# A transformer layer with routed experts on one core: shared chunks split 12 and 4 around the routed ones, and the final norm moved into the experts' block

## The chip, the core and the metric

One core of a Trainium2 chip runs the whole layer in one launch. The metric is device time in microseconds; the median of three runs of the kernel before is 2378.51 us (2376.24 to 2379.26). The profiled execution took 2377.52 us, of which the trace's span covers 2375.8. Engines are named TensorE (PE in the profile, its weight loads PEld), VectorE (DVE), ScalarE (ACT), GpSimd (POOL) and Sync (SP), which here only issues DMAs.

## The reference

`x` is (4, 2048, 256) float32, so there are 8192 tokens of width 256. What is computed:

```python
x = x + layernorm(attention(layernorm(x)))          # 16 heads, prefix mask
t = layernorm(x)                                    # the tokens
scores = softmax(t @ gate_w.T); idx = top_k(scores + gate_b, 2)
cw = sum(one_hot(idx, 8) * scores[idx])
a = swiglu((t @ w1.T + b1) * (t @ w3.T + b3))       # for each of 8 experts, F = 256
routed = sum_e cw_e * (a_e @ w2_e.T + b2_e)
shared = swiglu((t @ sw1.T + sb1) * (t @ sw3.T + sb3)) @ sw2.T + sb2
x = x + layernorm(routed + shared)
```

The products of the experts are float32 in accuracy: each is made of three passes, with operands split into a high and a low part (`_hi`, `_lo`).

## The kernel before

Tokens are worked on in chunks of 512 (`CH`), 16 in all (`NCH`), each as 4 tiles of 128. The stages are `prepare`, `project` (to 186 us), `attend` (to 1345), `attention_out` and `route` (to 1450), `experts` (to 2296) and `combine`.

`experts` runs 55 chunks (`NEC`), one step each, in one list for all engines: first 16 shared chunks (every token through the shared expert), then 39 routed ones (`ROUTED`), whose rows were sorted by expert. The steps are pipelined. In step c TensorE transposes the rows of chunk c+1 (`turn`, L293), makes three of four blocks of the hidden products (L1548), then the down product of chunk c-1 (L304), then the fourth block. ScalarE and VectorE evict the blocks, split the weights of the next chunk (L1587, L1654, L1663), its rows (L1591, L1659) and the activations (L1629, L1707). Each step reloads its expert's weights (`wraw`, 1.4 MB), in the shared chunks the same ones every time.

Beside the shared chunks GpSimd scatters the tokens to the sorted rows `rows_in` in DRAM: for each token chunk it writes the tails (expert weight and token number, L1462) behind the rows and issues 8 indirect DMAs (L1467) from two copies of the chunk, `xin` and `twin`. Sync loads the first routed chunk only when all are scattered; its queue is in order, so everything behind a wait stands too. A shared chunk's result is stored to `sums` by a plain DMA (L1637), and then routed results are added to it by indirect DMAs of GpSimd (L1485), four per chunk, each chunk after the one before has landed.

`combine` begins when everything is added. For each of 16 chunks Sync loads `sums` and `x1_scr`, VectorE measures mean and variance (L1786 to L1796), makes the inverse root in six small operations (L1801 to L1813), ScalarE normalizes (L1769), VectorE adds the residual (L1821) and GpSimd's queue stores (L1754).

## Time and profile before

| | us | how to read it |
|---|---|---|
| median of the runs | 2378.51 | 2376.24 to 2379.26 |
| profiled execution, its span | 2377.52, 2375.8 | all rows are of this execution, times from the span's start |
| TensorE busy | 2127.9 (90%) | over all stages; the table of stages says where it stands |
| ScalarE, VectorE, GpSimd busy | 1776.9, 1303.1, 700.5 | 75%, 55%, 29% of the span |
| last matmul ends | 2279.2 | 96.6 us before the end of the span |
| first load of the combine stage | 2296.21 | 79.6 us before the end |

A share of the whole span mixes stages with different limits. The rows below are read stage by stage: which engine is busy without a gap, and what ended the idle time of the others.

### The profile page before, as it was taken

The page shows a single profiled execution, that of the slowest core. Times are in us where ns is not written, and L with a number is a line of the kernel's source. Part 1 is how long each engine was busy: PE and PEld are TensorE (multiplying, and loading weights), DVE is VectorE, ACT ScalarE, POOL GpSimd, SP SyncE. Part 2 cuts the span into 40 slices and gives each one's busy share as a digit, 9 for nine tenths or more (in the row PEclk, how much of TensorE's full clock was granted, in tenths as well). Part 3 has the DMA queues.
Part 4 walks back from the last instruction along what each step waited for, and adds up shares of the span by engine and source line. Part 5 has one row for each costly group of instructions (what it writes and reads, how often), then busy time and mean ns, then how long its engine had stood idle before and what let it go on. Part 6 is the DMA issues. An engine that isn't in the chain of part 4 may idle for free. (4 is left out here: it accounts for less than half of the span.)

```text
span 2375.8 us, 37728 instructions
## 1 busy us (share of the span) xinstructions
PE 2127.9 (90%) x14197; PEld 1307.5 (55%) x14197; DVE 1303.1 (55%) x2070; ACT 1776.9 (75%) x2250; POOL 700.5 (29%) x700
## 2 busy tenths in 40 slices
PE   5995999999999999999995984999999999999920
PEld 4773333333333333333334873888888888888820
DVE  4663222222222222222224966988888888888848
ACT  4664999999999999999993762555566666666624
POOL 1111000000000000000001533887166666666631
PEclk9997999999999999999997976999999999999965
DMA  6886644555555544444503864888566767777558
GB/s 194 297 304 171 117 87 87 100 100 100 100 98 99 72 83 86 89 86 61 71 10 113 267 193 164 294 288 290 196 165 171 171 171 170 171 171 177 127 135 316
DMA packets 204264, 365.79 MB, mean 154 GB/s; under 512 B 18680, under 2 KB 141176, under 8 KB 195256
## 3 DMA queue, kind: packets, MB, share of 16 engines
q1 hardware_dynamic: 161084, 299.38, 46.9%
q0 software_dynamic: 34256, 55.20, 12.4%
q10 hardware_dynamic: 8748, 8.85, 1.2%
q8 instruction: 111, 1.82, 0.3%
q14 instruction: 65, 0.53, 0.1%
HBM read 219.81 MB, written 143.42 MB: 153 GB/s over the span
## 5 line engine op out<-in xcount | busy, mean ns | idle before, releaser
L959 ACT ACTIVATE att_prob<-att_scores 128x1024 f32<-128x1024 f32 (+2 forms) x1152 | 1022.6, 1047 | 38.2 <-PE att_scores L910 31.0
L929 PE MATMUL att_out<-att_prob,att_va 128*32 128x512 f32 (+3 forms) x5120 | 591.0, 543 | 14.7 <-DVE att_prob L991 14.7
L910 PEld LDWEIGHTS att_scores<-att_qs,att_ks 50*128 50x128 f32 x2560 | 213.1, 185 | 500.9 <-ACT att_prob L959 427.6
L910 PE MATMUL att_scores<-att_qs,att_ks 50*128 50x512 f32 (+3 forms) x2560 | 469.8, 433 | 18.3 <-DMA att_qs<-guard 17.0
L991 DVE SCALAR_TENSOR_TENSOR att_prob<-att_prob,att_tri 128x512 f32<-128x512 f32 x224 | 144.8, 688 | 613.4 <-ACT att_prob L959 613.4
L1485 POOL DMA_INDIRECT sums<-moe_y,moe_token x156 | 346.3, 2220 | 224.7 <-ACT moe_y L1641 189.1
L1548 PE MATMUL moe_ps<-moe_xt_hi,moe_w_hi 128*128 128x512 f32 x880 | 347.4, 395 | 0.0
L1548 PE MATMUL moe_ps<-moe_xt_hi,moe_w_lo 128*128 128x512 f32 x880 | 347.0, 394 | 0.0
L1548 PE MATMUL moe_ps<-moe_xt_lo,moe_w_hi 128*128 128x512 f32 x880 | 345.3, 392 | 0.0
L862 POOL DMA_DIRECT2D ctx_scr<-att_cout x64 | 48.3, 755 | 994.6 <-DVE att_cout L1009 954.1
L929 PEld LDWEIGHTS att_out<-att_prob,att_va 128*32 128x32 f32 x5120 | 111.3, 108 | 189.4 <-issue 96.3
L1614 ACT ACTIVATE moe_h<-moe_ps,moe_wb 128x512 f32<-128x512 f32 x220 | 148.7, 677 | 86.6 <-PE moe_ps L1548 80.3
L1548 PEld LDWEIGHTS moe_ps<-moe_xt_lo,moe_w_hi 128*128 128x128 f32 x880 | 165.7, 188 | 33.9
L1548 PEld LDWEIGHTS moe_ps<-moe_xt_hi,moe_w_lo 128*128 128x128 f32 x880 | 165.7, 188 | 33.7
L1548 PEld LDWEIGHTS moe_ps<-moe_xt_hi,moe_w_hi 128*128 128x128 f32 x880 | 165.7, 188 | 32.4
L1686 DVE SCALAR_TENSOR_TENSOR moe_u<-moe_ps,moe_wb,moe_h 128x512 f32<-128x512 f32 x220 | 164.0, 746 | 25.9 <-PE moe_ps L1548 25.9
L1622 ACT ACTIVATE moe_sig<-moe_u 128x1024 f32<-128x1024 f32 x55 | 58.5, 1064 | 124.1 <-DVE moe_u L1692 124.1
L1654 DVE TENSOR_TENSOR moe_w_lo<-moe_wraw,moe_w_hi 128x2048 fp32r<-128x2048 f32 x55 | 126.2, 2294 | 38.5 <-ACT moe_w_hi L1587 38.5
L1587 ACT ACTIVATE moe_w_hi<-moe_wraw 128x2048 fp32r<-128x2048 f32 x55 | 105.0, 1910 | 37.6 <-DMA moe_wraw<-w_experts 37.6
L304 PE MATMUL moe_psY<-moe_w_hi,moe_a_hi 128*128 128x256 f32 x440 | 123.5, 281 | 5.3 <-DVE moe_a_lo L1707 5.3
L1629 ACT ACTIVATE moe_a_hi<-moe_a 128x1024 fp32r<-128x1024 f32 x55 | 58.4, 1061 | 91.6 <-DVE moe_a L1703 91.6
L304 PE MATMUL moe_psY<-moe_w_lo,moe_a_hi 128*128 128x256 f32 x440 | 123.0, 280 | 0.0
(193 smaller groups left out, 3041.8 us busy)
## 6 DMA issues: line engine op xcount, KB each, us to landing
moe_wraw<-w_experts SPq DMA_DIRECT2D x55, 1412.0 KB, 6.6
qk_parts<-proj_qk SPq DMA_DIRECT2D x64, 512.0 KB, 4.2
att_qs<-qk_parts SPq DMA_DIRECT2D x180, 128.0 KB
att_ks<-qk_parts SPq DMA_DIRECT2D x180, 128.0 KB
rows_in<-att_zeros SPq DMA_DIRECT2D x13, 1548.0 KB, 21.0
moe_xin<-rows_in SPq DMA_DIRECT2D x39, 516.0 KB, 4.3
proj_xin<-x SPq DMA_DIRECT2D x16, 512.0 KB, 3.9
v_scr<-proj_va SPq DMA_DIRECT2D x16, 512.0 KB, 3.5
```

What stands on the lines that cost most here:

```text
L304: last = nc.tensor.matmul(psum, left[a][:, k, lsl], right[b][:, k, rsl], start=(i == 0), stop=(i == len(steps) - 1))
L910: last = nc.tensor.matmul(pss[e % SBUFS][:, h, at:at + CH - q0], ks[s][rows, half, kt * P:(kt + 1) * P], qs[s][rows, half, c * CH + q0:(c ...
L929: last = nc.tensor.matmul(pso[k % 2][strip, q0:], va[team % 2][:, kt, strip], prob[u % PBUFS][:, h, at:at + CH - q0], start=(kt == 0), sto ...
L959: nc.scalar.activation(prob[u % PBUFS][:, half * 2:half * 2 + 2, start:], pss[e % SBUFS][:, :, start:], ACT.Exp, scale=HD ** -0.5)\
L991: V.scalar_tensor_tensor(block, block, GREATEST, bcast(mask[:], 1, [P, TEAM, w]), op0=ALU.min, op1=ALU.mult).then_inc(masked, 1)
L1485: pool.indirect_dma_start(out=sums, out_offset=bass.IndirectOffsetOnAxis(token[k % TAILS][:, j:j + 1], 0), in_=y[s][:, j, :], in_offset=No ...
L1548: last = nc.tensor.matmul(psum[f % 2][:], wk(w[s][aa], which, k)[:, f * P:(f + 1) * P], xt[s][bb][:, k], start=(i == 0), stop=(i == 5))
L1587: nc.scalar.activation(w[s][0][:, 0:W13], wraw[s][:, 0:W13], ACT.Copy).then_inc(w_hi[s], 1)
L1614: nc.scalar.activation(h3[f % 2][:], ps3[f % 2][:], ACT.Identity, bias=wb[s][:, FB + f:FB + f + 1]).then_inc(h3_done[s], 1)
L1622: nc.scalar.activation(sig[:], u[:, 0:KT], ACT.Sigmoid, scale=ALPHA).then_inc(sig_done[s], 1)
L1654: V.tensor_tensor(w[s][1][:, 0:W13], wraw[s][:, 0:W13], w[s][0][:, 0:W13].bitcast(F32), ALU.subtract).then_inc(w_lo[s], 1)
L1686: V.scalar_tensor_tensor(u[:, f], ps1[f % 2][:], wb[s][:, f:f + 1], h3[f % 2][:], ALU.add, ALU.mult).then_inc(u_done[s], 1)
```

## The change

- The order of the chunks is now 12 shared ones (`FIRST`), the 39 routed ones, and 4 shared ones (51 to 54, for the last four token chunks). `AFTER` is 51.
- The weights of the shared expert are loaded and split for chunks 0, 1, 51 and 52 only. They stay in their two buffers; in chunks 2 to 11, 53 and 54 the load and the splits are left out.
- The scatter has its own buffers `moved` in place of `twin`, filled with two loads for each of 16 token chunks. The 16 are issued within the first 12 steps of Sync.
- The rows of `sums` that the last four shared chunks would have written are zeroed in advance, in the attention (2.6 MB of zeros where it was 0.5 MB). Results of chunks 51 to 54 stay in SBUF, in the free weight buffers (`kept_result`), and GpSimd adds them to the loaded sums (`add_kept`).
- `combine` is gone. Its work is in the experts' block, in pairs of chunks (`PAIRS` 8, in a ring of 4 buffers). The statistics of pairs 0 and 1 stand in the last two steps, the rest behind them. The norm works in place, the residual is added by GpSimd (`residual`), and Sync stores.
- The attention's weights give their SBUF free before the experts' block.

```diff
+FIRST = 12
+AFTER = FIRST + ROUTED
...
-                        sp.dma_start(sums[T:, :].rearrange("(p r) d -> p r d", p=P), zeros[:, 0:TPC, 0:D])\
-                            .then_inc(z_stored, 16)
+                        for i in range(2):
+                            at = FIRST * CH + i * P * SR
+                            sp.dma_start(sums[at:at + P * SR, :].rearrange("(p r) d -> p r d", p=P), zeros[:, 0:SR, 0:D])\
+                                .then_inc(z_stored, 16)
...
+        moved = ph.sb2("moved", [P, 2, TPC, RW])
...
+        loads = [c for c in range(NEC) if c < 2 or FIRST <= c < AFTER + 2]
+
+        def new_weights(c):
+            return c in loads
+
+        def loads_to(c):
+
+            return sum(1 for d in loads if d <= c and d % 2 == c % 2)
...
+        def kept_result(c):
+
+            s = c % 2
+            at = (c - AFTER) // 2 * TPC * D
+            return wraw[s][:, at:at + TPC * D].rearrange("p (j d) -> p j d", j=TPC)
...
+                def add_kept(p):
+                    pool.wait_ge(acc_loaded[p % RING], (p // RING + 1) * 16)
+                    for i in range(2):
+                        c = ROUTED + 2 * p + i
+                        n, s = divmod(c, 2)
+                        pool.wait_ge(y_biased[s], n * 2 + 2)
+                        nc.gpsimd.tensor_tensor(acc[p % RING][:, i], acc[p % RING][:, i], kept_result(c), ALU.add)\
+                            .then_inc(y_added, 1)
+
+                def residual(p):
+                    pool.wait_ge(x1_loaded[p % RING], (p // RING + 1) * 2 * 16)
+                    for i in range(2):
+                        pool.wait_ge(normed, p * PT + (i + 1) * TPC)
+                        nc.gpsimd.tensor_tensor(acc[p % RING][:, i], acc[p % RING][:, i], x1[p % RING][:, i], ALU.add)\
+                            .then_inc(done, 1)
+
+                for p in range(PAIRS):
+                    residual(p)
+                    if FIRST // 2 <= p + 3 < PAIRS:
+                        add_kept(p + 3)
...
+                def load_moved(i):
+                    n, s = divmod(i, 2)
+                    sp.wait_ge(scattered[s], n * each)
+                    for r in range(2):
+                        sp.dma_start(moved[s][:, r, :, 0:D], tok_ch[i]).then_inc(moved_loaded[s], 16)
+
+                def load_x1(p):
+                    for i in range(2):
+                        sp.dma_start(x1[p % RING][:, i], x1_scr[2 * p + i]).then_inc(x1_loaded[p % RING], 16)
+
                 for c in range(NEC):
                     n, s = divmod(c, 2)
                     sp.wait_ge(turned[s], n)
-                    if c < NCH:
-                        sp.wait_ge(scattered[s], n * each)
+                    if c < FIRST:
                         sp.dma_start(xin[s][:, :, 0:D], tok_ch[c]).then_inc(x_loaded[s], 16)
-                        sp.dma_start(twin[s][:, :, 0:D], tok_ch[c]).then_inc(twin_loaded[s], 16)
+                        for i in range(c * NCH // FIRST, (c + 1) * NCH // FIRST):
+                            load_moved(i)
+                    elif c < AFTER:
+                        k = c - FIRST
+                        if k == 0:
+                            for d in range(2):
+                                sp.wait_ge(scattered[d], NCH // 2 * each)
+                        if k >= 2:
+                            sp.wait_ge(token_done, k - 1)
+                            sp.wait_ge(wgt_done, k - 1)
+                        sp.dma_start(xin[s][:], rin_ch[k]).then_inc(x_loaded[s], 16)
                     else:
-                        if c == NCH:
-                            for d in range(2):
-                                sp.wait_ge(scattered[d], HALF * each)
-                        if c >= NCH + 2:
-                            sp.wait_ge(token_done, c - NCH - 1)
-                            sp.wait_ge(wgt_done, c - NCH - 1)
-                        sp.dma_start(xin[s][:], rin_ch[c - NCH]).then_inc(x_loaded[s], 16)
-                    sp.wait_ge(w_lo[s], n * 2)
-                    sp.wait_ge(w_bias[s], n)
-                    e = E if c < NCH else sp.value_load(expert_of[0:1, c:c + 1], min_val=0, max_val=E)
-                    sp.dma_start(wraw[s][:], w_experts[bass.ds(e, 1)].rearrange("a p w -> (a p) w"))\
-                        .then_inc(w_loaded[s], 16)
+                        sp.wait_ge(token_done, min(c - FIRST - 1, ROUTED))
+                        sp.wait_ge(wgt_done, min(c - FIRST - 1, ROUTED))
+                        sp.dma_start(xin[s][:, :, 0:D], tok_ch[c - ROUTED]).then_inc(x_loaded[s], 16)
+                    if new_weights(c):
+                        sp.wait_ge(w_lo[s], (loads_to(c) - 1) * 2)
+                        sp.wait_ge(w_bias[s], loads_to(c) - 1)
+                        e = E
+                        if FIRST <= c < AFTER:
+                            e = sp.value_load(expert_of[0:1, c - FIRST + NCH:c - FIRST + NCH + 1], min_val=0, max_val=E)
+                        sp.dma_start(wraw[s][:], w_experts[bass.ds(e, 1)].rearrange("a p w -> (a p) w"))\
+                            .then_inc(w_loaded[s], 16)
+                    if FIRST + 4 <= c < FIRST + 4 + RING:
+                        load_x1(c - FIRST - 4)
+
+                def store(p):
+                    sp.wait_ge(done, 2 * p + 2)
+                    sp.dma_start(out_tiles[:, p * PT:(p + 1) * PT], tiles(acc[p % RING][:])).then_inc(stored[p % RING], 16)
+
+                for d in range(2):
+                    sp.wait_ge(added[d], len([c for c in range(FIRST, AFTER) if c % 2 == d]) * TPC * 16)
+                for p in range(PAIRS):
+                    if p >= RING:
+                        store(p - RING)
+                        load_x1(p)
+                        sp.wait_ge(stored[p % RING], p // RING * 16)
+                    sp.dma_start(tiles(acc[p % RING][:]), sum_tiles[:, p * PT:(p + 1) * PT])\
+                        .then_inc(acc_loaded[p % RING], 16)
+                for p in range(PAIRS - RING, PAIRS):
+                    store(p)
...
+                def roots(p):
+                    act.wait_ge(var_done, p + 1)
+                    nc.scalar.activation(std[p % 2][:], var[p % 2][:], ACT.Sqrt).then_inc(std_done, 1)
+
+                def norm(p, halves):
+                    act.wait_ge(shift_done, p + 1)
+                    rows_of = tiles(acc[p % RING][:])
+                    for i in halves:
+                        for j in range(i * TPC, (i + 1) * TPC):
+                            nc.scalar.activation(rows_of[:, j], rows_of[:, j], ACT.Identity,
+                                                 bias=shift[p % 2][:, j:j + 1], scale=rstd[p % 2][:, j:j + 1])\
+                                .then_inc(normed, 1)
...
+                        if c == NEC - 1 and 1 <= f <= 2:
+                            norm(0, (f - 1,))
...
+                    if c >= NEC - 2:
+                        roots(c - NEC + 2)
...
+                for p in range(1, PAIRS):
+                    norm(p, range(1))
+                    if p + 1 < PAIRS:
+                        roots(p + 1)
+                    norm(p, range(1, 2))
...
+                    c = 2 * n + s
+                    if c < AFTER:
+                        wait_kept(dve, n, s)
+                        to = y[s]
+                    else:
+                        dve.wait_ge(w_lo[s], loads_to(c) * 2)
+                        dve.wait_ge(w_bias[s], loads_to(c))
+                        to = kept_result(c)
...
+                def measure_rows(p, i):
+                    dve.wait_ge(acc_loaded[p % RING], (p // RING + 1) * 16)
+                    if p >= FIRST // 2:
+                        dve.wait_ge(y_added, 2 * (p - FIRST // 2) + i + 1)
+                    if p >= 2:
+                        dve.wait_ge(mv_done, (p - 1) * PT)
+                    for j in range(TPC):
+                        V.bn_stats(stats[p % 2][:, i * TPC + j], acc[p % RING][:, i, j]).then_inc(stats_done, 1)
...
+                        if f == 0 and c == NEC - 1:
+                            invert(0)
...
+                        if f >= KT and c >= NEC - 2:
+                            measure_rows(c - NEC + 2, f - KT)
...
+                    if c >= NEC - 2:
+                        measure_end(c - NEC + 2)
                     if nxt is None:
+                        invert(1)
+                        measure(2)
...
-def combine(nc, sum_ch, x1_scr, out_ch):
...
+                for p in range(2, PAIRS):
+                    invert(p)
+                    if p + 1 < PAIRS:
+                        measure(p + 1)
```

Sync before the first routed chunk, in the kernel before (rows and weights of shared chunk 15, then of routed chunk 16; a digit behind a name is the buffer):

```order
L1506 DMA moe_xin1<-tokens 128x4x256
L1507 DMA moe_twin1<-tokens 128x4x256
L1519 DMA moe_wraw1<-w_experts 128x2824
L1515 DMA moe_xin0<-rows_in 128x4x258
L1518 TENSOR_LOAD keep_expert_of
L1518 ISA x2
L1519 ISA
L1519 DMA moe_wraw0<-w_experts 128x2824
```

and in the changed kernel (Sync's steps 11 and 12, the first routed chunk is 12):

```order
L1586 DMA moe_xin1<-tokens 128x4x256
L1576 DMA moe_moved0<-tokens 128x4x256 x2
L1576 DMA moe_moved1<-tokens 128x4x256 x2
L1597 DMA moe_xin0<-rows_in 128x4x258
L1607 TENSOR_LOAD keep_expert_of
L1607 ISA x2
L1608 ISA
L1608 DMA moe_wraw0<-w_experts 128x2824
```

The shared weights' load has gone, and two more token chunks are loaded for the scatter directly ahead of the first routed chunk's rows.

VectorE, step 1 (shared chunk 1 of 16) of the kernel before:

```order
L1686 SCALAR_TENSOR_TENSOR moe_u<-moe_ps1_0,moe_wb1,moe_h30 128x512
L1654 TENSOR_TENSOR moe_w0_lo<-moe_wraw0,moe_w0_hi 128x2048
L1686 SCALAR_TENSOR_TENSOR moe_u<-moe_ps1_1,moe_wb1,moe_h31 128x512
L1692 TENSOR_SCALAR moe_u<-moe_u 128x1024
L1659 TENSOR_TENSOR moe_xt0_lo<-moe_psT,moe_xt0_hi 128x1024
L1696 TENSOR_TENSOR moe_sig<-moe_sig,moe_u 128x1024
L1686 SCALAR_TENSOR_TENSOR moe_u<-moe_ps1_0,moe_wb1,moe_h30 128x512
L1670 TENSOR_TENSOR moe_y0<-moe_psY0,moe_wb0 128x512
L1670 TENSOR_TENSOR moe_y0<-moe_psY1,moe_wb0 128x512
L1686 SCALAR_TENSOR_TENSOR moe_u<-moe_ps1_1,moe_wb1,moe_h31 128x512
L1700 TENSOR_SCALAR moe_u<-moe_u 128x1024
L1703 SCALAR_TENSOR_TENSOR moe_a<-moe_u,moe_sig 128x1024
```

and the same step now:

```order
L1878 SCALAR_TENSOR_TENSOR moe_u<-moe_ps1_0,moe_wb1,moe_h30 128x512
L1878 SCALAR_TENSOR_TENSOR moe_u<-moe_ps1_1,moe_wb1,moe_h31 128x512
L1886 TENSOR_SCALAR moe_u<-moe_u 128x1024
L1797 TENSOR_TENSOR moe_xt0_lo<-moe_psT,moe_xt0_hi 128x1024
L1890 TENSOR_TENSOR moe_sig<-moe_sig,moe_u 128x1024
L1878 SCALAR_TENSOR_TENSOR moe_u<-moe_ps1_0,moe_wb1,moe_h30 128x512
L1817 TENSOR_TENSOR moe_y0<-moe_psY0,moe_wb0 128x512
L1817 TENSOR_TENSOR moe_y0<-moe_psY1,moe_wb0 128x512
L1878 SCALAR_TENSOR_TENSOR moe_u<-moe_ps1_1,moe_wb1,moe_h31 128x512
L1896 TENSOR_SCALAR moe_u<-moe_u 128x1024
L1899 SCALAR_TENSOR_TENSOR moe_a<-moe_u,moe_sig 128x1024
```

The two operations on the weights (`w_lo` from `wraw`) are gone; all others stand as they did.

GpSimd behind the last indirect add of the changed kernel, where the kernel before has only 16 stores of `out`:

```order
L1560 TENSOR_TENSOR moe_acc1<-moe_acc1,moe_x1_1 128x1024 x2
L1560 TENSOR_TENSOR moe_acc2<-moe_acc2,moe_moved0 128x1024 x2
L1560 TENSOR_TENSOR moe_acc3<-moe_acc3,moe_moved1 128x1024 x2
L1553 TENSOR_TENSOR moe_acc2<-moe_acc2,moe_wraw1 128x1024
L1553 TENSOR_TENSOR moe_acc2<-moe_acc2,moe_wraw0 128x1024
L1560 TENSOR_TENSOR moe_acc0<-moe_acc0,moe_x1_0 128x1024 x2
L1553 TENSOR_TENSOR moe_acc3<-moe_acc3,moe_wraw1 128x1024
L1553 TENSOR_TENSOR moe_acc3<-moe_acc3,moe_wraw0 128x1024
L1560 TENSOR_TENSOR moe_acc1<-moe_acc1,moe_x1_1 128x1024 x2
L1560 TENSOR_TENSOR moe_acc2<-moe_acc2,moe_moved0 128x1024 x2
L1560 TENSOR_TENSOR moe_acc3<-moe_acc3,moe_moved1 128x1024 x2
```

Twenty additions of 128x1024 are new on GpSimd: 16 with the rows to be added in `x1` or `moved`, and four of kept results, which stand between the residuals of pairs 3, 4 and 5.

## Rows read from the trace of the kernel before

Columns of a timeline: start in us, length in us, engine, line, operation, tiles written and read, shapes, count, and in brackets the idle time before it and what ended it.

**Rows 1.** stages, all engines: window, length, busy us (count) per engine, PEclk, DMA, GB/s

```profile
1420.00:1466.00 46.00, 5.78 (x13) 2.83 (x14) 29.19 (x51) 4.28 (x5) 8.58 (x14) 0.50 0.31 114
1700.00:2240.00 540.00, 540.00 (x2953) 464.91 (x2953) 482.33 (x518) 356.01 (x510) 336.64 (x210) 1.00 0.69 171
2296.00:2376.00 80.00, 0.00 (x0) 0.00 (x0) 63.34 (x256) 36.24 (x81) 12.23 (x16) 0.50 0.89 315
```

**Rows 2.** timeline of TensorE, transposes: start, length, line, operation, count, idle before

```profile
1465.95 1.30 PE L293 MATMUL moe_psT<-keep_ident,moe_xin 128*128 128x128 f32 x5 [9.13 <-DVE moe_xt_lo L1659]
1625.96 1.03 PE L293 MATMUL moe_psT<-keep_ident,moe_xin 128*128 128x128 f32 x8
2240.00 1.03 PE L293 MATMUL moe_psT<-keep_ident,moe_xin 128*128 128x128 f32 x8
```

**Rows 3.** timeline of GpSimd, scatter of the tokens

```profile
1456.39 0.19 POOL L1462 COPY moe_xin<-keep_tails 128x8 f32<-128x8 f32 x1 [34.74 <-DMA moe_twin<-tokens]
1469.77 0.21 POOL L1462 COPY moe_xin<-keep_tails 128x8 f32<-128x8 f32 x1
1470.38 0.98 POOL L1467 DMA_INDIRECT rows_in<-moe_xin,keep_slot  x1 [0.28 <-POOL moe_twin L1462]
1471.67 0.96 POOL L1467 DMA_INDIRECT rows_in<-moe_xin,keep_slot  x1 [0.30 <-issue]
1481.29 0.53 POOL L1462 COPY moe_xin<-keep_tails 128x8 f32<-128x8 f32 x1
1545.20 2.96 POOL L1467 DMA_INDIRECT rows_in<-moe_twin,keep_slot  x1 [0.30 <-DMA moe_twin<-tokens]
1562.59 0.60 POOL L1462 COPY moe_xin<-keep_tails 128x8 f32<-128x8 f32 x1
1671.99 1.75 POOL L1467 DMA_INDIRECT rows_in<-moe_twin,keep_slot  x1 [0.30 <-issue]
1679.39 0.19 POOL L1474 COPY moe_wgt<-moe_xin 128x4 f32<-128x4 f32 x1 [5.65 <-DMA moe_xin<-rows_in]
```

**Rows 4.** short stretches, as rows 1: start of the stage, combine

```profile
1465.00:1470.00 5.00, 4.05 (x14) 3.60 (x15) 1.40 (x2) 0.00 (x0) 4.08 (x6) 0.50 0.55 214
1470.00:1475.00 5.00, 5.00 (x24) 4.09 (x23) 2.84 (x2) 4.39 (x5) 3.81 (x5) 1.00 0.58 139
2310.00:2330.00 20.00, 0.00 (x0) 0.00 (x0) 18.45 (x79) 9.93 (x24) 3.93 (x5) 0.50 1.01 340
```

**Rows 5.** timeline of VectorE, beside the GpSimd row of 1545.20

```profile
1545.04 2.29 DVE L1654 TENSOR_TENSOR moe_w_lo<-moe_wraw,moe_w_hi 128x2048 fp32r<-128x2048 f32 x1 [0.44 <-ACT moe_w_hi L1587]
```

**Rows 6.** timeline of GpSimd, last indirect add of chunk 52

```profile
2263.83 2.05 POOL L1485 DMA_INDIRECT sums<-moe_y,moe_token  x1 [0.30 <-issue]
```

**Rows 7.** line L1485, all 156 indirect adds, to landing

```profile
DMA to landing us min/median/max: 3.6/5.3/7.8
```

**Rows 8.** timeline of the combine stage, several engines

```profile
2296.21 0.36 SPq L1745 DMA_DIRECT2D comb_acc<-sums  x1
2296.22 1.28 ACT L1762 ACT_TABLE_LOAD   x1 [14.54 <-PEq L83]
2302.36 0.18 DVE L1801 RECIPROCAL comb_root<-comb_std 128x4 f32<-128x4 f32 x1 [0.27 <-ACT comb_std L1762]
2303.37 0.16 DVE L1813 SCALAR_TENSOR_TENSOR comb_shift<-comb_mv,comb_rstd 128x4 f32<-128x4 f32 x1
2370.09 0.75 POOL L1754 DMA_DIRECT2D out<-comb_res  x1 [1.94 <-DVE comb_res L1821]
```

**Rows 9.** groups of instructions: count, busy us, mean ns, idle before

```profile
L1769 ACT ACTIVATE comb_nrm<-comb_acc,comb_shift,comb_rstd 128x256 f32<-128x256 f32 x64 | 33.0, 586 | 0.2 <-issue 0.2
L1786 DVE BATCH_NORM_STATS2 comb_stats<-comb_acc 128x6 f32<-128x256 f32 x64 | 22.4, 412 | 20.1 <-DMA comb_acc<-sums 20.1
L1821 DVE TENSOR_TENSOR comb_res<-comb_nrm,comb_x 128x1024 f32<-128x1024 f32 x16 | 19.6, 1225 | 2.0 <-DMA out<-comb_res 2.0
L218 POOL MEMSET prep_zeros<- 128x1024 f32 x1 | 1.0, 952 | 0.0
```

262 lines of the change are left out of this document (110 added, 152 removed).

## The prediction

> **What bounds the kernel now.** I read the table of stages first [rows 1]. From 1466 us to the end of the experts' stage TensorE is never idle (540.00 us busy out of 540 from 1700 on), at a granted clock of 1.00, the upper of its two levels (2.4 GHz). Before that it stands nearly still while the routing is worked out (5.78 us busy in 46), and after it, in the combine stage, it does nothing for 80 us. So the kernel has a full stretch that only less matmul work could shorten, and two gaps. The change leaves every matmul in place. It can win in the second gap, and it can lose by tearing a hole into the full stretch.
>
> The starts of the transposes give the pace of the full stretch [rows 2]. TensorE transposes the rows of chunk c+1 at the start of step c. Step 0 starts at 1465.95, step 11 at 1625.96, step 53 at 2240.00: 160.0 us for 11 steps (14.55 each) and 614.0 for 42 (14.6 each). I use these three times as fixed points.
>
> Beside TensorE, GpSimd scatters the tokens to the experts' sorted rows, 8 indirect DMAs for each of 16 chunks [rows 3]. It begins at 1456.39 and its last one ends at 1673.74; the first routed chunk's rows are loaded only after that and are there at 1679.39, 5.65 us later. TensorE turns them at the start of step 15, at 1625.96 + 4 x 14.6 = 1684. The scatter is off the critical path by 5 us, no more. This is the number to keep in mind.
>
> **The part that can lose: routed chunks start four steps earlier.** Sync loads routed chunk 12 only when all 16 token chunks are scattered, and TensorE needs it at the start of step 11, not 15. The order of instructions shows nothing on Sync between the last `moved` load and that load. So the time at which the scatter ends now sets the time at which TensorE goes on.
>
> - Start. The first token chunk is loaded three times in front of the first weights, where it was twice: 0.5 MB more, at 350 GB/s (an estimate from 340 GB/s in [rows 4] with all DMA engines busy) 1.5 us. GpSimd starts at 1457.9, step 0 at 1467.4 and step 11 would start at 1627.5.
> - Pace of the scatter. Token loads no longer wait for TensorE's turns in a way that binds (load i stands at Sync's step 0.75i, which waits for a turn at about 1424 + 10.9i, and waits for the scatter of chunk i-2, over at about 1448 + 11.6i, which is later), so GpSimd runs at its own pace. In the first eight chunks that is (1562.59 - 1456.39)/8 = 13.3 us [rows 3]. The floor is 8 x 0.96 us with 0.30 between them and 0.6 for the two tails (1469.77 to 1470.38): 10.4. The rest is blocking: the indirect DMA of 1545.20 took 2.96 us instead of 0.96; it began 0.16 us after VectorE's 2.29 us operation on the weights, and ended 0.83 us after it [rows 3, 5]. Once a chunk this costs 2.0. The change drops exactly that operation in steps 1 to 10, because the shared weights stay. Some requests will run into another operation instead, so I take 1.7 off: 11.6 us. Bounds are 10.4 (nothing blocks) and 13.3 (nothing gained).
> - Sum. Chunks 0 and 1 still meet weight preparation and take 1481.29 - 1456.39 = 24.9 us as before; 1457.9 + 24.9 + 14 x 11.6 = 1645.2; less 2 because VectorE stands still during the last two chunks, plus 5.65 to have the rows: 1648.9. TensorE has stood since 1627.5: 21.4 us. After a stand its clock is at 0.50 (the level of 1.2 GHz) for some 5 us, as at the start of the stage [rows 4]: 2.5 us of work lost. With the 1.5 of the start: **+25.4 us**. At a pace of 10.4 it is +11, at 13.3 it is +51.
>
> On this the Trainium skill speaks twice. SBUF — State Buffer, "Who interferes with whom", says that a VectorE instruction with two SBUF inputs holds up a GpSimd one that reads SBUF, for its whole length; but it also infers that tensor_tensor leaves descriptor generation alone. By the first sentence the pace falls as I have it; by the second the weight operations would not be the cause, the pace would stay at 13.3 and the whole would come out near 2397. The trace sides with the first: the 2.96 us.
>
> The weights of chunk 12 are issued about 1.4 us after its rows and must be there when ScalarE has evicted the first block after the stand; I count nothing for them, and up to 3 us if they are late. Fourteen weight loads and their splits that go away are worth nothing by themselves, since TensorE is full beside them. Zeroing 2.1 MB more of `sums` falls into the attention, on Sync's queue behind the loads of the work that comes next; nothing, at most 2.
>
> **The part that wins: the last norm.** I measure from the start of step 53 (A = 2240.00). The kernel before ends at A + 135.8.
>
> - The sums can be read when the last routed chunk is added. Chunk 52's last indirect add began at 2263.83, took 2.05 and lands 5.3 later [rows 6, 7]: 2271.2. Routed work now ends two chunks earlier: 2271.2 - 29.2 = A + 2. So just two steps of TensorE, not four, hide anything of the new work; the other two shared chunks are gone before the sums are complete.
> - Four loads of 1.05 MB at 350 GB/s, 3.0 us each: there from A + 7 to A + 17. Pair 0 is measured inside step 53 (8 x 0.41 [rows 9]) and normalized inside step 54 (8 x 0.59). ScalarE's square root now sits between the steps and changes its table, back for the sigmoid and again: 1.28 us each [rows 8]. It waits for VectorE's variance first. Estimates from these durations: step 54 starts at A + 14.6; 8 for the end of step 53's work on VectorE, the variance, the table and the root, 10 for the inverse, the table changes and the norm between the evictions, 1.9 for the last addition (below): pair 0 is done at A + 34.5. The last chunk's own work on VectorE ends at A + 39 by the same count; variance, root, inverse, norm and addition, 11 in all: pair 1 at A + 50.
> - From there Sync goes round: store a pair, load its x1, wait for the store, load the next sums: 3 x 1.05 MB = 9.0 us a pair. Sums of pairs 5, 6, 7 are there at A + 62, 71, 80.
> - The residual and the kept results are added on GpSimd, 128x1024 float32, which the trace of before does not have. The nearest rows are a memset of this size on GpSimd, 0.95 us, and VectorE's own addition, 1.23 [rows 9]. If two inputs are read one after the other it is 2 x 0.95 = 1.9; three passes, 2.9, is the upper end. I take 1.9.
> - After pair 7's sums: two kept additions 3.8, statistics 3.3 + 1.0, the inverse root 1.2 (2302.36 to 2303.53, [rows 8]), norm 4.7, the last residual 1.9: A + 96. The last store took 5.7 us before (2370.09 to the end at 2375.8 [rows 8]); for twice the size 6: A + 102. GpSimd's additions and VectorE's small two-input operations block each other as above; 3 us. A + 105.
>
> So the end comes 135.8 - 105 = **31 us** earlier. Bounds: 38 (additions 0.95, no blocking, somewhat faster DMA) and 22 (2.9 and 8 us of blocking). The DMA floor lies under this: the combine stage moved 315 GB/s on average [rows 1], 25 MB in all, and 21 MB of it are still to move after A + 2.
>
> The Trainium skill has a price for the addition that the trace lacks: GPSIMD Engine Reference, "Elementwise — side-by-side cycle accounting", gives 4497 ns for 2048 elements, so an estimate of 2.25 us here. By it the end would be 2 us later; no run yet shows it.
>
> **Sum.** +25.4 - 31 = -5.6. The profiled execution has a span of 2375.8 and took 2377.5, 1 us under the median of 2378.5. 2377.5 - 5.6 = 2371.9; I forecast 2372.
>
> **Rivals.**
> - The scatter keeps 13.3 us a chunk (other traffic or the instructions themselves set it). The hole is then 47 us and the change slower: 2377.5 + 51 - 31 = 2397. It decides from a pace of about 12.0 on, where loss and gain are even. For it: over all 16 chunks the pace is even 13.6 ((1673.74 - 1456.39)/16 [rows 3]). Against: the later ones were held back by TensorE's turns, and the blocked instruction is plain.
> - The scatter falls to its floor. Hole 7 us, +11 in all, 2357. For it: VectorE has a third less to do that blocks. Against: the other two-input operations remain.
> - GpSimd and VectorE block each other in the last norm. Each pair has six small operations in a row on VectorE; if each waits for a 1.9 us addition, a pair costs up to 11 us where 1.2 were counted, and the gain of 31 shrinks to some 20: 2383. For it: [rows 3, 5], where one waits for the other. Against: GpSimd has pauses while DMA is the slower.
> - The early steps hide all of the norm, as if the sums were ready at step 51: another 29 us, 2343. Against it stands the wait for the last adds.
>
> **How the numbers follow.** Forecast 0.55 (2360 to 2384 by itself), unchanged pace 0.12, floor 0.15, blocking at the end 0.13, the rest 0.05. The range reaches from 2354 to 2394; it leaves out most of the unchanged pace and the last rival. This kernel's runs tell 0.2% (4.8 us) from no change. Of the forecast's 0.55, 0.30 is faster, 0.18 same, 0.07 slower; the floor is faster, the unchanged pace slower, the blocking 0.05 same and 0.08 slower, the rest 0.03 and 0.02. Together 0.48, 0.23, 0.29.
>
> **What would show it.** The transposes of chunk 12 start near 1649 after an idle of about 21 us ended by the DMA of its rows, and the clock is at 0.50 behind it. The tails' copies on GpSimd lie 11 to 12 us apart, and no indirect DMA takes 2.96 us between chunks 2 and 10. The first `acc` load is issued 2 us after step 53 starts, the span ends some 105 us after that start. GpSimd's additions take near 1.9 us. If TensorE has no idle before chunk 12, or the scatter's pace is over 13, or the end lies more than 120 us behind step 53, the forecast is wrong at that step.

## The result, and the profile after

The changed kernel takes 2421.65 us (2420.76 to 2424.06, 4 runs) against 2377.38 beside it: ratio 1.0191, interval 1.0173 to 1.021. The forecast was 2372 with a range of 2354 to 2394. The change makes the kernel slower by 1.7 to 2.1%, and the time is outside the range.

I read TensorE's transposes first, against [rows 2] (timeline of the changed kernel; start, length, idle before in brackets):

```profile
1466.26 1.94 PE L297 MATMUL moe_psT<-keep_ident,moe_xin 128*128 128x128 f32 x8 [10.25 <-DVE moe_xt_lo L1797]
1495.49 1.04 PE L297 MATMUL moe_psT<-keep_ident,moe_xin 128*128 128x128 f32 x8
1558.09 1.04 PE L297 MATMUL moe_psT<-keep_ident,moe_xin 128*128 128x128 f32 x8
1699.20 1.03 PE L297 MATMUL moe_psT<-keep_ident,moe_xin 128*128 128x128 f32 x8
2313.24 1.04 PE L297 MATMUL moe_psT<-keep_ident,moe_xin 128*128 128x128 f32 x8
```

These are the starts of steps 0, 2, 3, 11 and 53. Step 0 is 0.3 us later than before, step 11 is 73.2 later, step 53 is 73.2 later. From step 11 on nothing more is lost. From step 53 to the end of the span it is 2422.3 - 2313.2 = 109.1 us, where it was 135.8. So 73.2 - 26.7 = +46.5: that is the whole difference of the two profiled executions (2424.06 - 2377.52).

The loss is not one hole. Step 2 alone takes 62.6 us in place of 14.6, step 6 30.5. Stages, to be held against [rows 1, 4] (window, length, busy us and count of TensorE, its weight loads, VectorE, ScalarE, GpSimd, then granted clock, DMA share, GB/s):

```profile
1480.00:1500.00 20.00, 16.52 (x93) 14.03 (x91) 11.69 (x14) 6.70 (x10) 15.79 (x19) 0.98 0.61 192
1500.00:1540.00 40.00, 17.67 (x46) 13.09 (x47) 4.69 (x5) 1.82 (x3) 30.95 (x39) 0.67 0.73 237
1540.00:1560.00 20.00, 10.06 (x39) 8.46 (x39) 7.14 (x10) 3.93 (x5) 4.86 (x6) 0.57 0.19 66
1560.00:1600.00 40.00, 40.00 (x221) 34.50 (x220) 27.85 (x32) 16.01 (x20) 19.64 (x24) 1.00 0.62 201
1600.00:1640.00 40.00, 29.50 (x121) 22.00 (x120) 16.53 (x20) 8.77 (x12) 22.70 (x27) 0.79 0.59 196
1700.00:2240.00 540.00, 540.00 (x2955) 465.03 (x2953) 481.78 (x517) 354.27 (x505) 327.58 (x206) 1.00 0.69 176
```

TensorE, VectorE and ScalarE stand together, while GpSimd goes on scattering. Which of them holds the others? A piece of TensorE's timeline, in the down product of step 2, names none (the first five lines follow each other, then two are left out):

```profile
1536.56 0.41 PE L308 MATMUL moe_psY<-moe_w_hi,moe_a_lo 128*128 128x256 f32 x1
1538.13 0.28 PE L308 MATMUL moe_psY<-moe_w_hi,moe_a_hi 128*128 128x256 f32 x1 [1.16 <-issue]
1540.93 0.37 PE L308 MATMUL moe_psY<-moe_w_lo,moe_a_hi 128*128 128x256 f32 x1 [2.52 <-issue]
1543.73 0.37 PE L308 MATMUL moe_psY<-moe_w_hi,moe_a_lo 128*128 128x256 f32 x1 [2.43 <-issue]
1546.53 0.37 PE L308 MATMUL moe_psY<-moe_w_hi,moe_a_hi 128*128 128x256 f32 x1 [2.43 <-issue]
1551.61 0.42 PE L308 MATMUL moe_psY<-moe_w_hi,moe_a_hi 128*128 128x256 f32 x1
1551.83 0.41 PE L308 MATMUL moe_psY<-moe_w_lo,moe_a_hi 128*128 128x256 f32 x1
```

These matmuls belong to one product, with no wait between them. Four of them start 2.80 us apart, where they come one in 0.21 before and behind. "issue" says that the profile names nothing that held them. The evictions of the same time (the reading of finished blocks out of PSUM), ScalarE's and then VectorE's:

```profile
1519.29 0.69 ACT L1741 ACTIVATE moe_h<-moe_ps,moe_wb 128x512 f32<-128x512 f32 x1 [11.64 <-remote]
1547.95 0.69 ACT L1741 ACTIVATE moe_h<-moe_ps,moe_wb 128x512 f32<-128x512 f32 x1 [27.98 <-remote]
```

```profile
1531.32 0.75 DVE L1878 SCALAR_TENSOR_TENSOR moe_u<-moe_ps,moe_wb,moe_h 128x512 f32<-128x512 f32 x1 [22.37 <-remote]
1551.57 0.75 DVE L1878 SCALAR_TENSOR_TENSOR moe_u<-moe_ps,moe_wb,moe_h 128x512 f32<-128x512 f32 x1 [19.50 <-remote]
```

The operand that VectorE's eviction at 1531.32 takes from ScalarE was written at 1519.98, and for the 11 us between no releaser is named. "remote" stands for another core, an unknown queue, or a semaphore that was raised long after the instruction that raises it is recorded as ended. My first reading was that the three engines had finished inputs and that their own instructions reached them late; I called this **late instructions**, and the expectations below use that name. The trace contradicts it. It also records when each semaphore was raised, and the four evictions above start right behind the raise that they wait for:

| eviction | recorded end of TensorE's last matmul for it | semaphore raised | late by |
|---|---|---|---|
| ScalarE, 1519.29 | 1503.12 | 1519.21 | 16.1 |
| VectorE, 1531.32 | 1507.47 | 1531.13 | 23.7 |
| ScalarE, 1547.95 | 1509.88 | 1547.92 | 38.0 |
| VectorE, 1551.57 | 1511.26 | 1551.48 | 40.2 |

ScalarE had its instruction: its wait for the first of these is recorded from 1506.59, and lasted 12.65 us. What came late was TensorE's report that a product is done. ScalarE's and VectorE's own raises, where recorded, follow the end of their operation by 0.01 us, and TensorE's stands end just behind such an operation: the eviction of 1519.29 ends at 1519.97, that of 1531.32 at 1532.07.

```profile
1520.03 0.80 PE L1657 MATMUL moe_ps<-moe_xt_hi,moe_w_hi 128*128 128x512 f32 x1 [8.77 <-ACT moe_h L1741]
1532.12 0.80 PE L1657 MATMUL moe_ps<-moe_xt_hi,moe_w_hi 128*128 128x512 f32 x1 [9.17 <-issue]
```

So the engines wait for each other in a circle, and GpSimd, which waits for none of TensorE's products here, goes on until its token rows are missing. Six matmuls lie between the second and the third report of the table, (1547.92 - 1531.13)/6 = 2.80 us each, the distance at which new ones start at the same time; but twelve that are recorded as started between 1520.03 and 1534.42 were reported at 1551.56 and 1551.63, 0.15 us behind the report before them at the most. Twelve take 2.7 us even at full clock (one in 0.23), so for these at least the report was late and not the work. The ends of matmuls in a profile are modelled, so how far each product was itself late is not shown. I call the condition **late signals** from here on.

It parts the profiles without a doubtful case. From 1466 to 1720 us the kernel before has all 120 of TensorE's raises within 0.2 us of a recorded end. The changed kernel has 32 of 114 later than that, and none of ScalarE's 69 or VectorE's 49. (Some raises are not in the record there, 20 of TensorE's 134.) Why the reports are late no run here shows.

The tail, to be held against [rows 6, 8, 9] (timelines of Sync and GpSimd, then groups from 2313 us on with count, busy us, mean ns, idle before):

```profile
2311.45 6.09 SPq L1624 DMA_DIRECT2D moe_acc<-sums  x4
2347.48 0.38 SPq L1615 DMA_DIRECT2D out<-moe_acc  x1
2364.10 0.39 SPq L1615 DMA_DIRECT2D out<-moe_acc  x1
```

```profile
2384.88 4.64 POOL L1553 TENSOR_TENSOR moe_acc<-moe_acc,moe_wraw 128x1024 f32<-128x1024 f32 x2 [7.58 <-DMA moe_acc<-sums]
2394.08 4.63 POOL L1553 TENSOR_TENSOR moe_acc<-moe_acc,moe_wraw 128x1024 f32<-128x1024 f32 x2
2410.06 6.43 POOL L1560 TENSOR_TENSOR moe_acc<-moe_acc,moe_moved 128x1024 f32<-128x1024 f32 x3 [2.31 <-ACT moe_acc L1722]
```

```profile
L1560 POOL TENSOR_TENSOR moe_acc<-moe_acc,moe_x 128x1024 f32<-128x1024 f32 x8 | 18.8, 2355 | 45.4 <-ACT moe_acc L1722 45.4
L1560 POOL TENSOR_TENSOR moe_acc<-moe_acc,moe_moved 128x1024 f32<-128x1024 f32 x8 | 17.3, 2173 | 9.2 <-ACT moe_acc L1722 9.2
```

### The profile page after: what moved, and what is told of

Same layout as the page of the kernel before. It is cut to its first block and busy times, and to the rows that moved or that the text cites. A ratio compares the mean times of both kernels' runs of the same rounds, so it can differ in the third digit from the quotient of the medians.

```text
span 2422.3 us, 37433 instructions
## 1 busy us (share of the span) xinstructions
PE 2150.1 (89%) x14197; PEld 1319.3 (54%) x14197; DVE 1256.1 (52%) x1974; ACT 1746.9 (72%) x2208; POOL 703.3 (29%) x704
## 5 line engine op out<-in xcount | busy, mean ns | idle before, releaser
L1657 PE MATMUL moe_ps<-moe_xt_hi,moe_w_hi 128*128 128x512 f32 x880 | 354.7, 403 | 29.1 <-ACT moe_h L1741 15.4
L1657 PE MATMUL moe_ps<-moe_xt_hi,moe_w_lo 128*128 128x512 f32 x880 | 352.3, 400 | 4.1 <-issue 4.1
L1657 PE MATMUL moe_ps<-moe_xt_lo,moe_w_hi 128*128 128x512 f32 x880 | 350.8, 399 | 1.8 <-issue 1.5
L1657 PEld LDWEIGHTS moe_ps<-moe_xt_hi,moe_w_hi 128*128 128x128 f32 x880 | 169.2, 192 | 66.4 <-issue 21.4
L1515 POOL DMA_INDIRECT rows_in<-moe_moved,keep_slot x128 | 132.0, 1031 | 38.9 <-issue 36.9
L308 PE MATMUL moe_psY<-moe_w_hi,moe_a_lo 128*128 128x256 f32 x440 | 123.6, 281 | 6.0 <-issue 6.0
```

The source lines that it names most:

```text
L308: last = nc.tensor.matmul(psum, left[a][:, k, lsl], right[b][:, k, rsl], start=(i == 0), stop=(i == len(steps) - 1))
L1515: pool.indirect_dma_start(out=rows_in, out_offset=bass.IndirectOffsetOnAxis(slot[:, r, t:t + 1], 0), in_=moved[s][:, r, j, :], in_offset=N ...
L1657: last = nc.tensor.matmul(psum[f % 2][:], wk(w[s][aa], which, k)[:, f * P:(f + 1) * P], xt[s][bb][:, k], start=(i == 0), stop=(i == 5))
```

## The experiments

They ran in five groups, each group on one chip with its own runs of the kernel before (medians 2377.9, 2378.4, 2378.9, 2377.4 and 2379.2 us). What that grouping hid is one of the lessons, so I tell them in their order. The starts of step 53 tell what the shared stage lost: 2240.0 is none. In the code cuts "..." marks lines of the same edit that are left out.

**Group 1.** What makes the engines stand? I asked it as "what makes the instructions late", with three theories that e1's expectation spells out: A, GpSimd's unbroken scatter; B, several token loads in a row on Sync; C, the amount of DMA traffic.

e1: weights loaded and split in every step.

```diff
-        loads = [c for c in range(NEC) if c < 2 or FIRST <= c < AFTER + 2]
+        loads = [c for c in range(NEC) if c < AFTER + 2]
```

> The changed kernel, with the shared expert's weights loaded and split in every step again, as in the kernel before (all else as changed). In the changed kernel TensorE loses 72 us between steps 2 and 11, in pieces, with no finished data missing. Theory A (free scatter): the engines get their instructions late because GpSimd issues its indirect DMAs without a pause, one chunk in 10.5 us, for longer than some 20 us; VectorE's weight operations (2.29 us) broke this up before. It expects here a pace of about 13.3 us a chunk, no stand inside steps 2 to 10, and one hole at chunk 12 of some 47 us: end near 2397. Theory B (bunched token loads): the four token loads in a row on Sync (10 us to issue) do it. It expects the stands in steps 2 and 6 as in the changed kernel, 60 us or more, whatever the pace: 2420 or later. Theory C (amount of DMA traffic): 1.4 MB more a step makes it worse, over 2430.

e2: GpSimd held up, behind each four indirect DMAs.

```diff
+PACE, PACES = 256, 6
...
+                        for i in range(PACES):
+                            nc.gpsimd.memset(slack[:], 0.0).then_inc(slack_set, 1)
...
```

> The changed kernel, with GpSimd held up on purpose in the scatter: behind each four of its indirect DMAs six small memsets of its own (128x256), estimated 0.3 us each, so some 3.5 us more a chunk. No DMA is added or removed. Theory A (free scatter starves the other engines of instructions) expects the stands of TensorE in steps 2 to 10 to go and one hole at chunk 12: pace 10.5 + 3.5 = 14 gives a scatter to 1456 + 16 x 14 = 1680, chunk 12 at 1686, hole 60 us and an end near 2410; if the memsets take less, earlier by 16 us for each us. Theory B (four token loads in a row) expects stands of tens of us in steps 2 and 6 as before, and 2430 or later.

e3: token loads of the scatter left out, but for the first two chunks, so its output is wrong.

```diff
                 def load_moved(i):
+                    if i >= 2:
+                        return
...
```

> The changed kernel with the scatter's token loads left out but for the first two chunks: GpSimd scatters the same two buffers again and again, so the rows are wrong and only the time is read. Sync has one 0.5 MB load a step in the shared chunks. Theory A (GpSimd's unbroken indirect DMAs) expects stands of TensorE in steps 1 to 9 that last as long as the scatter runs free, tens of us in all, and none after its end (16 chunks by 10.5 us: from 1456 to about 1630). Theory B (bunched token loads) expects TensorE at 14.6 us a step from step 0 to step 11, no stand over 2 us before chunk 12, and an end near 2355.

e4: the kernel before, keeping its shared weights.

```diff
-                    sp.wait_ge(w_lo[s], n * 2)
+                    if not new_weights(c):
+                        continue
+                    sp.wait_ge(w_lo[s], (loads_to(c) - 1) * 2)
...
```

> The kernel before, with one edit: the shared weights are loaded and split for chunks 0 and 1 only and kept (16 shared chunks first, token loads and combine as before). The token loads wait for TensorE's turns and for the scatter, so that GpSimd has a pause in every chunk: some 4 us at 14.6 a step and 10.5 of its own. Theory A expects no stand or at most small ones, since each chunk has its pause, and the time of the kernel before, 2377. If dropping the weight work alone starves the engines, TensorE loses tens of us here too and the end is over 2395. Theory B expects 2377 (two token loads a step, as before).

Measured: e1 2389.7, e2 2443.5, e3 2377.6, e4 2379.1 us. No late signals in any. What stands there has a named releaser: in e2 TensorE waits 38 us for its token rows and 45.4 for the rows of chunk 12, because Sync's queue is in order and waits for a scatter that takes 16.0 us a chunk (near 2410 was expected with 14). In e3 there is one hole (an end near 2355 was expected by theory B), and the transposes of chunk 12 and of step 53 are

```profile
1651.13 1.97 PE L297 MATMUL moe_psT<-keep_ident,moe_xin 128*128 128x128 f32 x8 [20.90 <-DMA moe_xin<-rows_in]
2267.27 1.03 PE L297 MATMUL moe_psT<-keep_ident,moe_xin 128*128 128x128 f32 x8
```

These are the numbers of the forecast's shared stage: it expected chunk 12 at 1649 after 21.4 us, and step 53 25.4 later than 2240.0; here it is 27.3. But e3 issues 4 of the 32 loads for the scatter, so that it agrees so well is partly luck; k1 below, with all of them and no late signals, has the hole too and is 34.2 late. e4 tests the pace, with 16 shared chunks first as before. The tails' copies of chunks 0 and 9 (GpSimd's timeline):

```profile
1458.45 0.19 POOL L1469 COPY moe_xin<-keep_tails 128x8 f32<-128x8 f32 x1 [34.74 <-DMA moe_twin<-tokens]
1562.68 0.54 POOL L1469 COPY moe_xin<-keep_tails 128x8 f32<-128x8 f32 x1
```

Nine chunks in 104.2 us are 11.6 each, in the kernel before 13.3 for eight [rows 3]. The pace term was right in size. At this point I believed that theory B (bunched token loads) or A was being singled out.

**Group 2.** Splits and loads apart, and 14 chunks first.

f1: split each step, without a load (`splits_to` counts them).

```diff
-                    if not new_weights(2 * n + s):
+                    if 2 * n + s >= AFTER + 2:
...
```

> The changed kernel, with the shared weights split anew in every step from the copy that lies in SBUF, but not loaded again. So ScalarE and VectorE have the work of the kernel before (VectorE's 2.29 us operation among it), and Sync and the DMA engines that of the changed kernel. The run with loads and splits lost no time to late instructions; this one tells which of the two did it. Theory D (VectorE's operations break up GpSimd's scatter, and that keeps the other engines fed): no stand of TensorE before chunk 12 for which no data is missing, pace about 12.2 us a chunk, a hole of some 30 us at chunk 12, end near 2385. Theory E (the weight DMAs on Sync's queue did it, by spacing the token loads or by occupying it): ScalarE, VectorE and TensorE wait for nothing visible as in the changed kernel, over 50 us between steps 2 and 11, end near 2420.

f2: loaded each step, not split.

```diff
+                    if 2 <= c < FIRST:
+                        sp.dma_start(wraw[s][:], w_experts[E:E + 1].rearrange("a p w -> (a p) w")).then_inc(w_again[s], 16)
...
```

> The other half: the shared weights are loaded again in each of the steps 2 to 11 (1.4 MB each, into the buffers that hold them already), and not split again. Theory D (VectorE's operations did it): late instructions and stands as in the changed kernel, end near 2420 or above. Theory E (the weight DMAs did it): none, pace 11.6, a hole of 20 to 25 us at chunk 12, end near 2378.

g1 and g2: 14 first, the norm behind the last step; g1 with reload and Sync's weights ahead of the scatter's loads.

```diff
-FIRST = 12
+FIRST = 14
...
-                        if f >= KT and c >= NEC - 2:
-                            measure_rows(c - NEC + 2, f - KT)
...
```

> A version meant to be faster than both. 14 shared chunks first and 2 behind; the shared weights are loaded and split in every step; Sync issues the weights ahead of the scatter's token loads; and no part of the norm stands in the last two steps, all pairs come behind them. Pace 12.2 as measured with the reload gives the end of the scatter at 1456 + 16 x 12.2 = 1651 and the rows of chunk 14 at 1657, where TensorE comes to it at 1466 + 13 x 14.62 = 1656: a hole of 0 to 5 us. The sums are complete two chunks earlier than in the kernel before, at A + 44 - 15 = about A + 29 to 31 (A: start of step 53), and then 21 MB move in 60 to 67 us, with some 15 around: A + 105 to 113 against A + 135.8. So 2347 to 2362 if theory A to E agree that the reload prevents late instructions; if FIRST or the order on Sync brings them back, over 2370.

> The same with 14 chunks first and the norm behind, but the shared weights kept as in the changed kernel, and Sync's order unchanged. Theory D (VectorE's weight operations keep the engines fed) and theory E (weight DMAs) both expect late instructions as in the changed kernel: tens of us lost in steps 2 to 12, 2380 to 2400. If they do not come, two token loads in one step less often (2 of 14 steps, not 4 of 12) are what counts, and the time is 2345 to 2360, the pace 11.6.

Measured: f1 2394.0, f2 2386.2, g1 2388.6 and g2 2364.0 us (2347 to 2362 and 2345 to 2360 were expected, so both missed), ratio of g2 0.9937 (0.992 to 0.9954). Again none has late signals, so f1 and f2, sent to say which half cured e1, say nothing on it. They do price the pace of the scatter (copies of chunk 0 to 15): 12.8 us with the splits, 12.2 with the loads, 12.3 with both in e1, 13.4 with both in g1, 11.8 in g2 with neither. The halves do not add up, but the single DMAs bear the forecast's cause out: of the 72 indirect DMAs of chunks 2 to 10, five to seven take over 2 us wherever the weights are split (kernel before, e1, f1, g1), the longest 2.97 to 2.98; without splits (e3, e4, f2, g2) none takes over 1.88. In g1 chunk 14 waits 22.3 us for its rows. The tail of g1 and g2 takes 120 us from step 53 where I expected 105 to 113: in g2 the DMA engines pause from 2283 to 2295 us, while the first pairs are still normed.

**Group 3.** The changed kernel again (h1, no edit), and three near it.

> The changed kernel unchanged, a second time. If the late instructions belong to the program (theory F: how its instructions lie and are fetched beside this order of DMAs), the stands come back in steps 2 and 6 with 48 and 16 us and the time is 2421. If they depend on chance from execution to execution (theory G), their places and sum differ and the time spreads between 2375 and 2430.

h2: the norm's edit of g2 with `FIRST = 12`, on ScalarE

```diff
-                        if c == NEC - 1 and 1 <= f <= 2:
-                            norm(0, (f - 1,))
...
```

and the like on VectorE.

> The changed kernel (12 shared chunks first, weights kept) with the norm taken out of the last two steps, as in the version with 14 that had no stand. Nothing is changed before step 53. If 12 chunks first, that is four token loads in every third step, make the instructions late, the stands of the changed kernel are here too: 72 us before chunk 12. Theory F (placement of the instructions) also allows them, but they may move. If there is no stand but the hole at chunk 12 (21 us), the end is near S53 = 2267 plus 105 to 115: 2372 to 2382.

h3: pairs of token loads in steps 0, 3, 6 and 9.

```diff
-                        for i in range(c * NCH // FIRST, (c + 1) * NCH // FIRST):
+                        for i in range(-(-c * NCH // FIRST), -(-(c + 1) * NCH // FIRST)):
```

> The changed kernel with the four steps that load two token chunks moved two steps ahead: 0, 3, 6 and 9 in place of 2, 5, 8 and 11. If the pairs of loads cause the late instructions (theory B), the stands move by two steps with them, tens of us in steps 3 to 7. If it is the placement of the instructions (theory F: Sync's own order hardly touches that of the other engines), they stay in steps 2 and 6 with 48 and 16 us. If they are gone altogether, the hole at chunk 12 alone is left, 21 us, and the end is near 2376.

h4: instructions shifted, with 24 more transposes, 20 copies of ScalarE and 20 memsets of VectorE in front of step 0.

```diff
+                    for i in range(3 if (n, s) == (0, 0) else 0):
+                        transposes(nc, psT, xin[s][:, :, 0:D], ident)
...
```

> The changed kernel with its instructions shifted: in front of the experts' first step TensorE repeats the transposes of chunk 0 three times (24 more), ScalarE copies and VectorE writes 20 single columns. It costs at most 2 us where TensorE stands anyway. DMAs and their order are the same. Theory F (where an engine's instructions lie against the blocks that are fetched) expects the stands to move or go, by more than 20 us of the 72. Theories B and A (loads, scatter) expect them unchanged: 2421 to 2424.

Measured: h1 2415.8 (2411.6 to 2420.8), h2 2427.6, h3 2418.6 (2403 and 2434), h4 2408.0 (2388 to 2411). All four have late signals (32 to 42 of TensorE's raises over 0.2 us late, none of ScalarE's or VectorE's), and places and sizes differ: what the longest step takes over 14.6 us is 29.7 in step 2 (h1), 32.5 in step 3 (h2), 35.9 in step 2 (h3), 32.2 in step 3 (h4), where it was 48.0 in step 2. So it is not bound to one instruction or one load.

**Group 4.** Does the pattern of loads decide?

k1 and k2: `range(...)` replaced by a table of loads a step, `[1] * 11 + [5]` for 12 chunks first, and `[1, 1, 2, 1, 1, 2, 1, ...]` for g2's 14.

> The changed kernel (12 first, weights kept), with one token chunk for the scatter loaded in each of the steps 0 to 10 and the last five in step 11, behind TensorE's own rows, in place of two in every third step. If the early steps with two token loads make the instructions late (theory B), there is no stand here but the one at chunk 12: 21 to 25 us, end near 2374 to 2380. If 12 shared chunks first with kept weights is enough whatever the pattern, 30 to 70 us are lost in steps 2 to 9 as in the four versions measured: 2405 to 2430.

> The version with 14 shared chunks first that had no stand (2364), with two token loads already in steps 2 and 5, where the versions with 12 have them, in place of 6 and 13. Theory B (early pairs): stands of 30 to 70 us come with late instructions, over 2390. If the pairs are innocent: 2364 again, within 4.

k3: g2 with the kept pair first.

```diff
+        order = [PAIRS - 1] + list(range(PAIRS - 1))
...
-                        c = ROUTED + 2 * p + i
+                        c = ROUTED + 2 * order[p] + i
...
```

> A better tail for the version with 14 chunks first: the pair of chunks whose results were kept in SBUF is normed first, not last. In that version's profile the last pair waited 10 us for its sums, then GpSimd's two additions of the kept results (4.6 us) stood between the load and the statistics, and the path from the last sums (2333.8) to the end took 26 us. A plain pair needs 2.7 + 0.6 + 1.3 + 4.1 + 2.3 + 5.7 = 17. The end comes 5 to 9 us earlier, 2355 to 2359. If DMA sets the end by itself, 2362 to 2364.

k4: a memset in place of each indirect DMA of the scatter, so its output is wrong.

```diff
-                            pool.indirect_dma_start(
...
+                            nc.gpsimd.memset(slack[:], 0.0).then_inc(scattered[s], 16)
...
```

> The changed kernel with the scatter's indirect DMAs left out: GpSimd writes a scratch tile of its own (128x1280, some 1.2 us) in the place of each, so the routed rows stay empty and only the shared stage is read. All loads of Sync stand as in the changed kernel. If the loads alone make the instructions late (theory B without the scatter), the stands are here as well, tens of us in steps 2 to 9. If it takes GpSimd's indirect DMAs beside them, there is no stand over 2 us before chunk 12.

Measured: k1 2385.0 (2374 to 2380 was expected), k2 2364.9, k3 2357.7 (0.9914, 0.9897 to 0.993), k4 2372.7 us in its one run; no late signals in any. In k1 TensorE waits 29.4 us for the rows of chunk 12. k2 has Sync's loads as h2 has them up to step 6, and loses under 1 us where h2 had lost 40 us from step 0 to the start of step 4. The two differ in the chip as well. I had not put the changed kernel into this group, so that k1 and k4 say as little on the cause as group 1.

**Group 5.** The changed kernel and the best version on one chip, the one of groups 1 and 4.

> The changed kernel once more, unchanged. The comparisons so far lie on several chips: all versions that lost time to late instructions ran on one chip in one group (and the changed kernel itself at first on a chip not noted), all that did not on two others. If the program alone decides (12 first, kept weights, pairs of token loads), this run takes 2410 to 2425 on whatever chip it lands, with late instructions. If the chip decides with it, then on a chip of the second kind it takes 2374 to 2382, with one hole of about 25 us before chunk 12.

> The best version so far (14 chunks first, weights kept, the pair with the kept results normed first), on the same chip as the changed kernel of this group. If the changed kernel shows late instructions here and this does not, the time is 2357 as before and the program decides; if both show them, this one is at 2375 or above and the chip decides for both. If neither does, 2357.

Measured: m1 2411.3 us (2407.9 to 2423.8), m2 2387.2 (2374.7 to 2393.3, 10 runs). m2 is k3's kernel, unchanged, on the chip with the same number, 29.5 us slower; and its ten runs do not reach down to k3's four (2354.6 to 2358.9). Windows of the same stretch, k3's and then m2's:

```profile
1540.00:1590.00 50.00, 50.00 (x273) 42.91 (x272) 34.02 (x40) 18.46 (x24) 39.47 (x46) 1.00 0.81 263
```

```profile
1540.00:1590.00 50.00, 30.91 (x123) 23.85 (x123) 15.47 (x19) 7.99 (x10) 27.89 (x34) 0.76 0.56 185
```

and from m2's table of waits for 1500 to 1700 us (in total, times, longest); k3's has no "remote":

```profile
DVE moe_u L1876 <- remote: 30.3, 5, 13.2
ACT moe_h L1742 <- remote: 23.5, 5, 9.5
```

By the raises 33 of TensorE's 143 are over 0.2 us late in m2, and none of 187 in k3. So neither the program alone nor the chip's number decides (whether it is the same chip is not on record). Late signals came in the first comparison and in groups 3 and 5, for every changed version that ran there (7 profiles, 32 to 42 late raises each), and in no profile of groups 1, 2 and 4 (12, no late raise in any). k3 and m2 are the one program that was profiled both with and without them. The kernel before took 2377.4 to 2379.2 in all of them. What differs between the groups (where a program lies in memory, what the rest of the chip does) these runs do not tell, so the cause stays open.

## Why the prediction was wrong

- **Start, +1.5.** 0.3 measured in the changed kernel; 2.2 to 3.7 in e3, e4 and k3. Small.
- **Shared stage, +25.4: the step that failed.** It was 73.2. The sum rested on a sentence ahead of it, "TensorE is never idle from 1466 on", taken over from the kernel before as a property of the stage. The row was true; that TensorE loses nothing but the hole at chunk 12 with another load on GpSimd and DMA was assumed, and no rival allowed for another loss there. In its place the runs showed late signals: TensorE's finished products are reported up to 40.2 us late, the evictions wait for the reports and TensorE for the evictions, 48.0 us in step 2 alone. Where the reports were in time the parts were near the forecast: pace 11.6 to 11.8 (forecast 11.6), chunk 12 at 1651.1 in e3 (1649), idle 20.9 (21.4). Step 53 is late by 27.3 in e3, 22.3 in k4, 34.2 in k1, and by 73.2, 62.8 (h1) and 61.5 (m1) in the changed kernel, so by e3 late signals cost it some 34 to 46 us. No run of the changed kernel itself escaped them, so its time without them is an estimate: 2240.0 + 27 + 109 + 1.7 = 2378 from e3 and the tail, and 7 more from k1, which took 2385.0.
- **Its bounds.** By the sum's own terms a pace of 10.4 gives +8.6 and one of 13.3 +49.2; the +11 and +51 leave out the 2 us for VectorE's rest. That changes nothing here.
- **"No indirect DMA of 2.96 us, copies 11 to 12 apart."** The first is so: the longest from chunk 2 to 10 takes 1.88. Copies lie 12.7, 11.9, 11.9, 10.4, 10.7, 10.5 and 10.5 apart to 1535.9, the last ones at the floor while VectorE is busy 4.69 us of 40.
- **Weights and splits that go away: 0.** e4 2379.1 against 2377.9 (ratio 0.9992 to 1.0015): right. In the changed kernel 12 loads go away (55 to 43), not fourteen. **Zeroing: 0.** Step 0 is not later than the start term says.
- **Tail, -31: measured -26.7.** Read from A = 2313.2: first sums issued at A - 1.8 (forecast A + 2); pair 0 stored at A + 34.2 (34.5), pair 1 at A + 50.9 (50); sums of pairs 6 and 7 there by A + 71.6 and A + 80.8 (71 and 80). The last addition ends at A + 103.2 (96, and 99 with the 3 for blocking), the end is A + 109.1 (105). The mis-sized terms are the blocking and GpSimd's addition, which takes 2.17 to 2.36 us in place of 1.9. The Trainium skill, GPSIMD Engine Reference, "Elementwise — side-by-side cycle accounting", whose price gave an estimate of 2.25, was the better one: the trace agrees with it to 0.11 us. But three additions behind pair 7's sums make just 1.1 us.
- **GpSimd and VectorE blocking in the norm** (a rival, 0.13): true, and on the path that ended last. VectorE's small operations on 8 columns, pair 6 and then one of pair 7:

```profile
2392.40 1.74 DVE L1852 TENSOR_TENSOR moe_root<-moe_root 128x8 f32<-128x8 f32 x1
2394.18 2.26 DVE L1854 TENSOR_TENSOR moe_root<-moe_root,moe_var 128x8 f32<-128x8 f32 x1
2396.47 2.27 DVE L1856 TENSOR_SCALAR moe_root<-moe_root 128x8 f32<-128x8 f32 x1
2398.77 2.26 DVE L1860 TENSOR_TENSOR moe_rstd<-moe_root 128x8 f32<-128x8 f32 x1
2401.07 2.26 DVE L1862 SCALAR_TENSOR_TENSOR moe_shift<-moe_mv,moe_rstd 128x8 f32<-128x8 f32 x1
2408.49 0.17 DVE L1854 TENSOR_TENSOR moe_root<-moe_root,moe_var 128x8 f32<-128x8 f32 x1
```

Beside eight of GpSimd's additions one behind another (2384.88 to 2403.30) five operations take 10.9 us, where they take 1.0 in pair 7: the 11 us a pair that the rival gave, but in one pair of eight. Pair 7's statistics start 4.5 us after its rows are ready, because VectorE is still on pair 6; with 0.9 in pair 7's variance that is 5.4 us of blocking where 3 were counted. The gain did not shrink to the rival's 20: pairs 2 to 4 lose at most 1.6 us each in their variance, and the others nothing.
- **The rival "unchanged pace" at 2397** was the nearest in time and false in its mechanism: the pace did fall where nothing else stood.

In the version that came out best the same two terms are traded: with 14 first the hole is gone (step 53 at 2240.4 in g2), the sums are ready later, the tail takes 120 (g2) or 113 (k3). It beats the kernel before by 0.9% in group 4 and is 0.3% slower (1.0008 to 1.0049) in group 5. I would carry it on only with the late signals understood.

## What to carry to other kernels

A bound engine is bound under the load it was measured with; when the change shifts what another engine or the DMA queues do beside it, give "it stands for a reason I have no row for" a chance and a width. Before you name the cause of a wait that has no releaser, put the recorded end of the instruction that it waits for beside the time at which its semaphore was raised: here that turned "instructions come late" into "reports of finished work come late". And put the kernel that shows an effect into every group of runs that is to explain its absence: three groups of careful edits here told nothing on the cause, because the effect was absent from the group.
